# A graph layer on one core: norms, row making, squares and biases laid out anew in the keys-and-values stage

## What is computed

```python
xn = _layernorm(x, axis=-1)                  # no gain or bias
k = split_heads(xn @ wk.T); v = split_heads(xn @ wv.T)      # 4 heads of 64
k = layer_norm(k, ln_k_g, ln_k_b); v = layer_norm(v, ln_v_g, ln_v_b)
kv = einsum('bhsd,bhse->bhde', k, v) / S
# message passing, h = xn
gate = sigmoid(silu(rbf @ W1 + b1) @ W2 + b2)
aggr = segment_sum(gate * h[src], dst)
upd = silu(concatenate([h, aggr]) @ U1 + c1) @ U2 + c2
x = x + h + upd + (q @ kv) @ wo.T + bo       # then x + experts(layernorm(x))
```

## Time and profile before

| | us |
|---|---|
| median of 3 runs (1099.18 to 1100.66) | 1100.58 |
| the profiled execution | 1099.37 |
| its span, first to last instruction | 1097.4 |
| PE busy / VectorE / ScalarE / POOL | 1042.6 / 886.2 / 690.1 / 750.6 |

### The profile page before, as it was taken

The page is one execution under the profiler, slowest core; times in us unless marked ns, Lnnn a source line. Parts: engine busy times, 40 slices in busy tenths (PEclk is TensorE's granted clock), DMA queues, the critical chain, the costliest instruction groups (busy, mean ns, idle before and its releaser), DMA issues.

```text
span 1097.4 us, 23714 instructions
## 1 busy us (share of the span) xinstructions
PE 1042.6 (95%) x7962; PEld 984.7 (90%) x7962; DVE 886.2 (81%) x1482; ACT 690.1 (63%) x1079; POOL 750.6 (68%) x703
## 2 busy tenths in 40 slices
PE   4897999999999999999999999998899999999996
PEld 2465899999999999999999999997699999999995
DVE  7877898888999988888888983487777777777773
ACT  2563667766666666666666654655367777777763
POOL 5447777777777777777777776540157777777765
PEclk9998999999999999999999999998899999999998
DMA  7211444445445544454444430216168989888980
GB/s 244 78 59 32 137 140 143 141 140 140 142 143 143 142 145 144 141 144 143 137 141 142 143 98 22 78 54 204 40 187 236 228 227 229 222 226 222 238 204 9
DMA packets 118528, 159.75 MB, mean 146 GB/s; under 512 B 20568, under 2 KB 91052, under 8 KB 118444
## 3 DMA queue, kind: packets, MB, share of 16 engines
q0 software_dynamic: 31104, 66.28, 26.1%
q1 hardware_dynamic: 86780, 91.60, 25.6%
q10 hardware_dynamic: 560, 0.79, 0.3%
HBM read 142.42 MB, written 18.17 MB: 146 GB/s over the span
## 4 chain that ended last, share of the span: by engine, by line
POOL 40%; PE 37%; issue 13%; DVE 8%; DMA 1%; ACT 1%; POOLq 0%; DVEq 0%; SPq 0%; ACTq 0%
POOL big L623 20%; POOL hgx L623 19%; PE ps L1897 16%; PE ps L1909 8%; PE ps L1752 3%; PE ps L1625 2%; PE ps L1764 2%; PE ps L1777 1%; PE ps L1884 1%; DVE st L1049 1%; PE ps L1634 1%; PE ps L1832 1%; PE ps L1635 1%; PE ps L1618 1%; DMA x_nodes<-in_x 1%
## 5 line engine op out<-in xcount | busy, mean ns | idle before, releaser
L1697 PE MATMUL ps<-fr 128*128 128x256 f32 x2352 | 306.9, 287 | 3.2 <-DVE fr L1111 3.2
L1697 PEld LDWEIGHTS ps<-fr 128*128 128x128 f32 x2352 | 289.4, 192 | 4.1 <-DVE fr L1111 4.1
L623 POOL DMA_INDIRECT big<-xn_rows,srcs x200 | 221.0, 1105 | 61.3 <-issue 61.3
L623 POOL DMA_INDIRECT hgx<-xn_rows,srcs x192 | 211.0, 1099 | 58.5 <-issue 58.5
L789 ACT ACTIVATE h1f<-ps,b 128x512 f32<-128x512 f32 x196 | 124.1, 684 | 165.4 <-PE ps L1651 164.3
L1708 PEld LDWEIGHTS ps<-oh,big 128*128 128x128 f32 x1568 | 189.8, 191 | 8.8 <-DVE big L1247 0.6
L1897 PE MATMUL ps<-fr 128*128 128x256 f32 x1536 | 190.3, 283 | 1.6 <-issue 1.3
L1897 PEld LDWEIGHTS ps<-fr 128*128 128x128 f32 x1536 | 186.7, 192 | 2.4 <-issue 2.4
L1708 PE MATMUL ps<-oh,big 128*128 128x96 f32 x1568 | 188.2, 273 | 0.5 <-DVE big L1256 0.5
L1111 DVE TENSOR_TENSOR fr<-h1f,fr 128x1024 fp32r<-128x1024 f32 x98 | 120.0, 1225 | 50.5 <-ACT fr L792 50.5
L695 POOL DMA_INDIRECT out<-xnT,idx x60 | 112.0, 1867 | 40.8 <-issue 31.8
(11 more groups left out here) (241 smaller groups left out, 1413.6 us busy)
## 6 DMA issues: line engine op xcount, KB each, us to landing
big<-in_w SPq DMA_DIRECT2D x128, 256.0 KB, 4.1
rbf<-in_rbf SPq DMA_DIRECT2D x98, 256.0 KB, 2.9
big<-in_w SPq DMA_DIRECT2D x32, 512.0 KB, 4.4
xn_rows<-xn SPq DMA_DIRECT2D x26, 128.0 KB, 2.5
big<-xn_rows,srcs POOLq DMA_INDIRECT x200
xn_rows<-hgx SPq DMA_DIRECT2D x24, 128.0 KB, 2.3
hgx<-xn_rows,srcs POOLq DMA_INDIRECT x192, 3.2
out<-x_nodes SPq DMA_DIRECT2D x6, 512.0 KB
```

The source lines that it names most:

```text
L623: pool.indirect_dma_start(hg[i % HB][:, s, :], None, xn_d[:, :], bass.IndirectOffsetOnAxis(srcs[:, col:col + 1], 0))\
L1697: last = mm(ps[:, 2 + 4 * p + s // 2, (s % 2) * D:(s % 2 + 1) * D], h1s[p][a][:, c, s * P:(s + 1) * P], W2s[b][:, c, :], start=c == 0 and ...
```

## The change

- **Norms.** Five batches of 2, 4, 6, 6 and 7 tiles (`LNCUT`) instead of three of 4, 6 and 15, placed by the tables `ROWSAT` and `NORMAT`. Each batch also makes -mean/std (`nmx`). The sum that the centring needs stands behind the first two rows; the centring on POOL is in two halves, and PE's first projection waits for each half.
- **Rows.** ScalarE makes xn of tiles 2 to 17 (`norm_xn`), VectorE those of 0, 1 and 18 to 24.
- **Squares.** Four buffers instead of two.
- **ScalarE's other work.** Clears start at t = 15 instead of 10, and the last ones stand behind the loop; W1 and W2 are rounded at t = 13 and 14. VectorE splits them at t = 16 and 17.
- **Tail.** From t = 25 VectorE scales the keys ahead of the sums of squares, seeds and steps; the edge features are split at 27 and 29 instead of both at 30; `up(0)` stands after the sum of tile 19 instead of 22.
- **Biases on POOL.** The first 13 tiles' biases stand behind the scaled values of tiles 3 to 15; those of the other 12 stand in the edge loop, each behind the gathers of one of the chunks 12 to 23. The last part of the mark of uncovered edges (`edges_marked`) stands behind the scaled values of tile 1.

```diff
+LNCUT = (0, 2, 6, 12, 18, NT)
+ROWSAT = {0: (6, 12), 2: (12, 14), 3: (14, 16), 4: (16, 18), 9: (18, 20), 10: (20, 22), 11: (22, NT)}
+NORMAT = {0: 2, 8: 3, 12: 4}
+ACTXN = (LNCUT[1], LNCUT[4])
+SQB = 4
+CLEARAT = 15
+BIASED = 13
...
             for t in range(NT):
                 scale_v(t)
-                add_biases(t)
+                if t == 1:
+                    edges_marked()
+                if 3 <= t < 3 + BIASED:
+                    add_biases(t - 3)
...
                         pool.indirect_dma_start(hg[i % HB][:, s, :], None, xn_d[:, :],
                                                 bass.IndirectOffsetOnAxis(srcs[:, col:col + 1], 0))\
                             .then_inc(s_hg[i % HB], 16)
+                    if type(n0) is int and 12 <= i < 12 + NT - BIASED:
+                        add_biases(BIASED + i - 12)
...
+            def norm_xn(t):
+                if not ACTXN[0] <= t < ACTXN[1]:
+                    return
+                act.wait_ge(s_ln, sum(t >= a for a in LNCUT))
+                if t >= XB:
+                    act.wait_ge(s_xnst[t % XB], t // XB * 16)
+                    act.wait_ge(s_tp, t - XB + 3)
+                act.activation(xn[t % XB], x[:, t, :], ACT.Identity, scale=rstd[:, t:t + 1], bias=nmx[:, t:t + 1])\
+                    .then_inc(s_xn, 1)
             copy_xt(0)
             copy_xt(1)
+            norm_xn(2)
             for t in range(NT):
+                norm_xn(t + 3)
                 if t + 2 < NT:
                     copy_xt(t + 2)
                 drain_kv(t)
-                if t > KLAG:
-                    clear(t - KLAG - 1)
...
+                if t >= CLEARAT:
+                    clear(t - CLEARAT)
...
             for t in range(NT + KLAG):
-                if t + 3 < NT:
-                    if t + 3 == 4:
-                        layer_stats(4, 6)
-                    if t + 3 == 10:
-                        layer_stats(10, NT - 10)
+                if ACTXN[1] <= t + 3 < NT:
+                    dve.wait_ge(s_xn, t + 3)
                     make_xn(t + 3, XB, s_xn, s_xnst, s_tp)
...
+                if t >= NT:
+                    scale_k(t - KLAG, (t - KLAG) % 2)
                 if 2 <= t < NT + 2:
-                    sum_sq(t - 2, t % 2)
+                    sum_sq(t - 2)
+                if t in ROWSAT:
+                    rows(*ROWSAT[t])
...
-                if t >= KLAG:
+                if t in NORMAT:
+                    norms(NORMAT[t])
+                if KLAG <= t < NT:
                     scale_k(t - KLAG, (t - KLAG) % 2)
```

More of the change, by code:

```diff
@@ L216, in gps_layer @@
         idx = [sb(f"idx{i}", [P, ET], i32) for i in range(2)]
-        sq = [h1f[:, i, :] for i in range(2)]
+        sq = [h1f[:, i, :] for i in range(2)] + [part(hgx, 1024 * i, 512) for i in range(2)]
+        nmx = part(hgx, 1760, NT)
         oflat = [oh[i][:, :, :].rearrange("p s w -> p (s w)") for i in range(2)]
@@ L572, in centre_wkv @@
                 link(pool.tensor_scalar(v_p[:, :], v_p[:, :], 1.0 / HD, None, ALU.mult))
-                pool.tensor_tensor(heads, heads, v_p[:, :].unsqueeze(2).to_broadcast([P, DC * 8, HD]), ALU.subtract)\
-                    .then_inc(s_cen, 1)
+                for c in range(DC):
+                    h = slice(c * 8, c * 8 + 8)
+                    pool.tensor_tensor(heads[:, h, :], heads[:, h, :],
+                                       v_p[:, h].unsqueeze(2).to_broadcast([P, 8, HD]), ALU.subtract).then_inc(s_cen, 1)
             def edge_tables():
@@ L769, in _ @@
                 drain_kv(t)
-                if t > KLAG:
-                    clear(t - KLAG - 1)
-            act.wait_ge(s_par, 16 * NPAR)
-            for dst, src in ((W1s[0], W1[:, :]), (W2s[0], W2[:, :, :])):
-                act.copy(dst, src).then_inc(s_whi, 1)
+                if t >= CLEARAT:
+                    clear(t - CLEARAT)
+                if t == 13:
+                    act.wait_ge(s_par, 16 * NPAR)
+                    act.copy(W1s[0], W1[:, :]).then_inc(s_whi, 1)
+                if t == 14:
+                    act.copy(W2s[0], W2[:, :, :]).then_inc(s_whi, 1)
+            for u in range(NT - CLEARAT, NT - KLAG):
+                clear(u)
             act.sem_inc(s_silu, 4)
-            act.wait_ge(s_sq, NT + 2)
+            act.wait_ge(s_sq, NT + SQB)
             def edges(n0, h0):
@@ L1045, in layer_stats, with norms @@
                 rsqrt(rstd[:, q], v, v_a[:, 0:n], v_b[:, 0:n])
+            def norms(k):
+                q = slice(LNCUT[k], LNCUT[k + 1])
+                layer_stats(LNCUT[k], LNCUT[k + 1] - LNCUT[k])
+                dve.scalar_tensor_tensor(nmx[:, q], mv[:, q, 0], -1.0, rstd[:, q], ALU.mult, ALU.mult)\
+                    .then_inc(s_ln, 1)
             def stats(t):
@@ L1125, in get_x @@
                 return stats(t)
-            for t in range(4):
+            for t in range(LNCUT[1]):
                 last = get_x(t)
+            link(last)
+            for t in range(LNCUT[1]):
+                last = moments(t)
+            link(last)
+            norms(0)
+            for t in range(LNCUT[1]):
+                make_xn(t, XB, s_xn, s_xnst, s_tp)
             dve.wait_ge(s_wkv, 16)
@@ L1131, in _, with weights_low @@
                 .then_inc(s_wsum, 1)
-            link(last)
-            for t in range(4):
-                last = moments(t)
-            link(last)
-            layer_stats(0, 4)
-            for t in range(3):
-                make_xn(t, XB, s_xn, s_xnst, s_tp)
-            def weights_low():
-                dve.wait_ge(s_whi, 2)
-                dve.tensor_tensor(W1s[1], W1[:, :], W1s[0].bitcast(f32), ALU.subtract)
-                dve.tensor_tensor(W2s[1], W2[:, :, :], W2s[0].bitcast(f32), ALU.subtract).then_inc(s_wlow, 1)
+            def weights_low(k):
+                dve.wait_ge(s_whi, k + 1)
+                halves, of = ((W1s, W1[:, :]), (W2s, W2[:, :, :]))[k]
+                dve.tensor_tensor(halves[1], of, halves[0].bitcast(f32), ALU.subtract).then_inc(s_wlow, 1)
             def rows(a, b):
@@ L1150, in rows @@
                 link(last)
+            rows(LNCUT[1], LNCUT[2])
+            norms(1)
             for t in range(NT + KLAG):
-                if t + 3 < NT:
-                    if t + 3 == 4:
-                        layer_stats(4, 6)
-                    if t + 3 == 10:
-                        layer_stats(10, NT - 10)
+                if ACTXN[1] <= t + 3 < NT:
+                    dve.wait_ge(s_xn, t + 3)
                     make_xn(t + 3, XB, s_xn, s_xnst, s_tp)
-                if t == 0:
-                    rows(4, 10)
+                if t >= NT:
+                    scale_k(t - KLAG, (t - KLAG) % 2)
                 if 2 <= t < NT + 2:
-                    sum_sq(t - 2, t % 2)
+                    sum_sq(t - 2)
+                if t in ROWSAT:
+                    rows(*ROWSAT[t])
                 if t >= 5 and t - 1 in KVCUT:
@@ L1166, in _ @@
                         kv_step(KVCUT.index(t - 1 - i) - 1, i)
-                if t >= KLAG:
+                if t in NORMAT:
+                    norms(NORMAT[t])
+                if KLAG <= t < NT:
                     scale_k(t - KLAG, (t - KLAG) % 2)
-                if 1 <= t < 7:
-                    rows(10 + 5 * (t - 1) // 2, 10 + 5 * t // 2)
                 if t == 14:
@@ L1176, in _ @@
                     dve.tensor_copy(flag[:, :], ps[:, 7, 0:1]).then_inc(s_flag, 1)
[L1177 to L1179 removed]
+                if t in (16, 17):
+                    weights_low(t - 16)
+                if t == NT + 2:
                     rbf_low(0, 0, 0)
+                if t == NT + 4:
                     rbf_low(0, 1, 1)
```

22 lines of the change are left out of this document (11 added, 11 removed).

## The result

| | before | after |
|---|---|---|
| median, us | 1100.42 (1099.18 to 1100.66, 5 runs) | 1163.50 (1151.29 to 1166.49, 5 runs) |
| profiled execution, its span | 1099.37, 1097.4 | 1151.29, 1149.3 |

The ratio is 1.0561, 95% interval 1.0504 to 1.0618: slower. The profiled execution of the changed kernel is the fastest of its five; the other four took 1162.87 to 1166.49. Where single executions of a kernel lie more than 1.5% over its fastest, its ratio leaves them out and the text names them.

A forecast was written before the change was run, and what follows sets the result against it. GpSimd's (POOL's) gathers bound the edge stage although PE looks full: 1099.4 - 12.4 (earlier start) + 20.5 (biases) + 46.6 (pace after chunk 23) - 0.2 = 1154 us. The range for all cases was 1088 to 1170.

The forecast's parts named there:

- the likeliest case: Edge loop stays at a slow pace behind the biases: 1154 us, own range 1118 to 1180, chance 0.45.
- The bound: Edge loop: POOL's row gathers set the end; every us POOL loses there comes out, however full PE looks.
- The pace after chunk 23: Edge loop behind the biases: 6.2 us a chunk, not 5.59, for 74 chunks; 46.6 us, bounds 23 to 75.
- one arrangement of the rows: Loop after chunk 23: L1111 holds the next chunk's first gather, the message the third; the fourth ends at about 6.2 us.
- The biases: Twelve behind the gathers of chunks 12 to 23: 1.7 us each, 20.5 in all, bounds 1.6 to 21.
- the gap of 0.68 us: POOL's queue: a gather behind a bias comes 0.68 us after it, not 0.30, so a bias adds 1.10.
- The start: Stages ahead of the edge loop: POOL's first gather 12.4 us earlier (8 to 15), at about 91.6.
- the first sum: First tiles of keys and values: first sum at about 37.5 instead of 43.8, 6 us gained (4 to 7.5).
- the middle: Keys-and-values stage from 43.8 to 87.0 us, PE-bound at 2.82 us a tile: 0 gained, at worst -1.5.
- the tail: Stretch from 87 to 104 us: 11.4 for 17, 5.6 gained (4 to 7), plus 0.8 without the last bias.
- B: Edge loop finds the good phase again after chunk 23, only the biases' price stays: 1101 us (1093 to 1108), chance 0.25.
- A: Biases fill POOL's waits in the loop, 0.13 to 0.5 us each, 4 in all: 1091 us (1086 to 1097), chance 0.30.

The follow-up runs named there:

- f1_none_in_loop: The changed kernel with no bias in the edge loop, the last three ahead of the first gather; 1097.14 us, ratio 0.9971.
- g1: The kernel before with 2 biases moved among the gathers, behind chunks 12 and 13; four executions: 1099.87, 1102.16, 1132.70 and 1160.12 us.
- f2: The kernel before with 12 biases moved behind the gathers of chunks 12 to 23; 1162.96 us, ratio 1.0583.
- g3: The changed kernel, biases still in the loop, with VectorE's hidden-layer rest and message each done in two halves; 1095.53 us, ratio 0.9978.
- h1: The changed kernel with all biases in the first stage, two a tile, and VectorE's two long loop operations in halves; 1093.04 us, ratio 0.9936.

## Why the prediction was right, and where it was not

Slower by a slow pace behind the biases, 1154 us, was forecast; the median is 1163.5, inside the range. The range of 1088 to 1170 held all three cases, so it tests little; the likeliest case's 1118 to 1180 is the test. (Its own bounds, 1.6 to 21 and 23 to 75, add up to 1111 to 1183.) That 1154 lies so near the profiled 1151.29 is luck in part: the start brought 7.5 us less than forecast, the pace cost 8.0 less, the biases 3.1 less, and smaller terms cancel too. By its steps:

**The bound was read rightly.** The edge stage ends at POOL's start plus POOL's time, though PE looked full: f1_none_in_loop and the changed kernel differ in POOL's queue alone, by 6%. That every us lost in the loop comes out at the end holds only once the lead is down to what the last message needs: g1's profiled execution lost 2.86 and still ended with before.

**The pace after chunk 23** was put at 6.2 and 46.6 us. In the profiled execution it is 446.39 / 73 = 6.12, 38.6 us. In f2 it is 6.27. The four longer executions of the changed kernel, some 12 us over the profiled one, would have about 6.28 if that pace is all that differs (12 / 73 = 0.17; no trace shows it). The forecast argued it from one arrangement of the rows: each message starts when its gather lands, L1111 holds the next chunk's first gather and the message the third. The trace bears out the first half: of the messages of chunks 24 to 96, 57 of 73 waited for their rows (70 in f2), so POOL is the pace and earns no lead back. The arrangement itself is not what ran: an L1148 held the first gather of 33 chunks and a message the third of 38, but both in one chunk only 6 times, and single chunks took from 5.0 to 7.9 us. The 6.12 is the mean of changing places, so the nearness of 6.2 owes something to luck. How a gather is held was nearly right too. The forecast wanted the operation on foot 0.13 us after the gather's start; it must have begun before the gather, for the one of 499.75 above, which starts 0.04 us ahead of an L1143, takes its 0.95.

**The biases** were put at 1.7 each, 20.5 in all; they cost 17.4, 1.45 each. The sum was nearly right for a wrong reason. POOL's timeline around two of them:

```profile
171.95 0.95 POOL L639 DMA_INDIRECT big<-xn_rows,srcs  x1 [0.31 <-issue]
172.93 1.78 POOL L568 TENSOR_TENSOR x_nodes<-x_nodes,cb 128x256 f32<-128x256 f32 x1
174.86 1.10 POOL L639 DMA_INDIRECT big<-xn_rows,srcs  x1 [0.16 <-issue]
...
180.47 0.74 POOL L568 TENSOR_TENSOR x_nodes<-x_nodes,cb 128x256 f32<-128x256 f32 x1
181.37 1.77 POOL L639 DMA_INDIRECT hgx<-xn_rows,srcs  x1 [0.16 <-issue]
```

The step that failed is the gap of 0.68 us behind an operation of that kind. Among gathers it is 0.16, and the bias itself starts 0.02 behind a gather. In the queue a bias takes 0.74 + 0.16 + 0.02 - 0.30 = 0.62 (g3: 0.58), not 1.10: 7.4 for twelve. What made up for it is that the 48 gathers of these chunks took 1.28 us in the mean, where they took 1.09 before: 8.9 in all. One bias was itself held up by 1.0.

**The start** was mis-sized: 12.4 us were forecast for the first gather (99.09 - 104.03 is 4.9), outside its bounds of 8 to 15. Term by term: the first sum at 39.91, 3.9 earlier, not 6; the middle 44.5 us for 43.2, near the bound of -1.5 and not 0; the tail (from the sum at 84.44 to the first gather) 14.65 for 17.0, so 2.4 and not 5.6 and 0.8. The timeline of the first tiles:

```profile
8.70 0.73 DVE L1097 TENSOR_SCALAR xn<-x_nodes,mv,rstd 128x256 f32<-128x256 f32 x2
...
12.21 3.75 PE L1666 MATMUL ps<-wkv,xnT 128*128 128x512 f32 x4 [1.92 <-POOL wkv L584]
...
17.61 3.62 PE L1666 MATMUL ps<-wkv,xnT 128*128 128x512 f32 x4
...
39.91 0.71 PE L1675 MATMUL ps<-oh 128*128 128x129 f32 x4 [2.84 <-DVE oh L1134]
```

The first projection began at 12.21, as forecast (12). But the second began at 17.61, not 16.5, and both took over 3.6 us, twice the 1.88 of later ones; the forecast counted 2.1 a tile from the second on. The slow second one is the miss: in g3_halves, whose first stage has the same instructions, it began at 17.35 and took 1.88, the third began at 19.37 and not 21.45, and the first sum came at 37.67, as forecast (37.5). The granted clock is given as 1.00 for both kernels there, so what slowed it stays open. The batch of norms that stands ahead of the first scaled keys (33.91 to 36.33) is not the miss: the first sum waited 2.84 us for the keys here, and 2.80 in g3_halves. In the tail the same operations ran at different clocks in these two kernels: the window of g3_halves over its tail, which starts with the same sum at 83.28, and then PE's first edge matmuls of the changed kernel and of g3_halves.

```profile
83.28:96.32 13.04, 10.49 (x59) 7.43 (x57) 10.59 (x26) 7.51 (x12) 6.21 (x9) 1.00 0.14 40
...
91.28 2.27 PE L1691 MATMUL ps<-fr 128*128 128x512 f32 x4
...
89.53 1.27 PE L1694 MATMUL ps<-fr 128*128 128x512 f32 x4
```

With the clock granted in full the tail is 13.0 us; with 0.88 it is 14.65. The forecast's 11.4 less its 0.8 is 10.6. PE had gone idle three times in 5 us ahead of the edge matmuls (0.27, 1.31 and 0.56 us) in both. So of the missing 7.5 us 2.1 lie ahead of the first sum (the slow projection), 1.3 in the middle and 4.0 in the tail, and 1.6 of these 4.0 go with the clock; the other 2.4 are missing at full clock too. Why one kernel kept it and the other did not stays open; the halves touch only the loop.

**The rivals.** That the good place is found again behind the biases (B, 0.25) did not happen in the profiled executions with twelve biases, and did in g1's with two, at a lead of 13.2. That a bias fills waits and costs under 0.3 us (A, 0.30) was wrong for this kernel: even with halves it cost 0.58. Its chance should have been lower, for even the forecast's own rows had 5.0 + 0.72 over 5.59.

**The end.** The forecast took nothing for the stretch from the last message on, and it took 3.8 us more. The slow scatter explains only a part: f2 has the same late message and the same scatter of 3.70 us, and takes 1.2 us more than before there.

## What to carry to other kernels

- An engine that issues gathers back to back, without waiting and without being waited for, can be the bound even when another engine is 95% busy. Before anything is put in its queue, compare its period (here 4 x (1.10 + 0.30) = 5.6) with the bound's (5.59): if they are equal, each us added beyond the lead that is left comes out at the end, and more. Waits for a third engine inside that period (0.59 here) need not be filled by the new work.
- A queue that keeps up only in one place against another engine is one disturbance from a slower pace: price it at a random place, from the operations that hold it, and look at the spread of the executions as well as at their median. Cutting the two holding operations in halves brought the loop back to 5.58 us a chunk and left no long execution among ten (g3) and four (h1), for some 0.15 us of VectorE a chunk (a halved L1148 takes 1.21 us to the start of the next operation, a whole one 1.13; the message 1.20 and 1.14).
